# The end of a state-space stage: three C products on VectorE, gate and projection in parts, the shift on GpSimd, statistics by pairs

## What is computed

```python
def _L1_attn_ref(x_in, W_in, W_x, W_dt, b_dt, A_log, D_param, W_out, ln_g, ln_b):
    xz = x_in @ W_in
    x, z = (xz[..., :D], xz[..., D:])
    ...
    dA = jnp.exp(jnp.einsum('bld,dn->bldn', delta, A))
    dBx = jnp.einsum('bld,bln->bldn', delta * x, B_ssm)
    def step(h, inp):
        dA_t, dBx_t, C_t = inp
        h = dA_t * h + dBx_t
        y_t = jnp.einsum('bdn,bn->bd', h, C_t)
        return (h, y_t)
    ...
    y = jnp.moveaxis(ys, 0, 1) + x * D_param
    y = y * jax.nn.silu(z) @ W_out
    res = y + x_in
    ...
    return (res - mu) * jax.lax.rsqrt(var + LN_EPS) * ln_g + ln_b

h = h + _L1_attn_ref(_layernorm(h, axis=-1), ...)
h = h + _L1_ffn_ref(_layernorm(h, axis=-1), ...)
```

## Time and profile before

| | us |
|---|---|
| median of 3 runs | 739.95 |
| lowest and highest | 738.63, 740.12 |
| the profiled execution | 738.0 |
| its span, first to last instruction | 736.2 |

### The profile page before, as it was taken

One profiled execution on the slowest core, in us unless ns is written; L12 is line 12 of the kernel. 1 busy time (PEld: TensorE's weight loads), 2 busy tenths in 40 slices (PEclk: granted clock), 3 DMA queues, 4 the chain that ended last, 5 costly groups with the idle time before them and its releaser, 6 DMA issues.

```text
span 736.2 us, 15971 instructions
## 1 busy us (share of the span) xinstructions
PE 673.4 (91%) x6442; PEld 522.6 (71%) x6489; DVE 345.0 (47%) x1039; ACT 256.0 (35%) x638; POOL 140.4 (19%) x109
## 2 busy tenths in 40 slices
PE   9898899899856698999988989999999998999997
PEld 6666688795433356876754679888886556998996
DVE  3328550006999876568578642211117762211113
ACT  0433354454633505563692212222220112222221
POOL 2000110001299900130050221111110040111110
PEclk9999999999999999999999999999999999999999
DMA  8981099916465230000002889999347047899923
GB/s 306 390 285 57 16 328 381 396 64 219 148 158 145 66 130 1 0 1 1 0 2 99 317 289 344 382 358 373 138 139 305 0 169 242 340 373 357 359 97 104
DMA packets 30196, 144.97 MB, mean 197 GB/s; under 512 B 4592, under 2 KB 14640, under 8 KB 23600
## 3 DMA queue, kind: packets, MB, share of 16 engines
q1 hardware_dynamic: 26352, 136.31, 50.9%
q0 software_dynamic: 2624, 6.71, 2.6%
q10 hardware_dynamic: 1152, 0.98, 0.4%
HBM read 133.19 MB, written 10.79 MB: 196 GB/s over the span
## 4 chain that ended last, share of the span: by engine, by line
PE 66%; DVE 12%; issue 10%; DMA 4%; ACT 3%; POOL 3%; SPq 1%; DVEq 0%; ACTq 0%; POOLq 0%
PE PS L592 62%; DVE arena L2219 5%; DMA y_slots<-arena 2%; PE PS L651 2%; SPq L436 1%; DMA gatew<-gate_w 1%; PE PS L615 1%; POOL arena L1659 1%; DMA arena<-bc_scratch 1%; DVE arena L2354 1%; POOL arena L1646 1%; POOL arena L1662 1%; ACT XT L1255 1%; PE PS L1049 0%; POOL arena L1654 0%
## 5 line engine op out<-in xcount | busy, mean ns | idle before, releaser
L592 PE MATMUL PS<-arena 128*64 128x64 f32 (+4 forms) x3090 | 249.3, 264 | 11.3 <-DVE arena L2357 3.1
L592 PEld LDWEIGHTS PS<-arena 128*64 128x64 f32 (+1 forms) x3090 | 210.9, 154 | 40.3 <-issue 14.9
L1982 DVE TENSOR_TENSOR arena<-arena,PS 128x384 f32<-128x384 f32 (+1 forms) x66 | 26.8, 407 | 175.5 <-ACT arena L1299 175.5
L592 PE MATMUL PS<-warm 128*128 128x512 bf16 (+2 forms) x306 | 74.6, 352 | 5.0 <-POOL warm L1586 1.3
L1299 ACT ACTIVATE arena<-PS 128x384 f32<-128x384 f32 (+1 forms) x66 | 27.2, 413 | 135.4 <-PE PS L592 135.4
L1629 POOL DMA_INDIRECT y_tok<-arena,yto x32 | 29.7, 928 | 195.8 <-ACT arena L1316 90.5
L1646 POOL TENSOR_TENSOR arena<-arena 128x1152 f32<-128x1152 f32 x16 | 56.4, 3522 | 31.7 <-DVE arena L2219 31.6
L592 PE MATMUL PS<-arena,ident 128*128 128x512 f32 (+1 forms) x128 | 38.0, 440 | 21.5 <-POOL arena L1646 21.5
L1616 POOL DMA_INDIRECT x_slots<-XHW,posu x25 | 24.2, 966 | 166.0 <-DVE posu L1896 159.3
L592 PEld LDWEIGHTS PS<-warm 128*128 128x128 bf16 (+1 forms) x353 | 31.8, 101 | 33.3 <-issue 4.8
L592 PE MATMUL PS<-arena,wsh 128*64 128x64 f32 (+3 forms) x680 | 50.7, 249 | 3.5 <-ACT arena L1291 2.4
(11 more groups left out here) (318 smaller groups left out, 933.7 us busy)
## 6 DMA issues: line engine op xcount, KB each, us to landing
arena<-w_moe SPq DMA_DIRECT2D x24, 2176.0 KB, 10.1
arena<-w_moe SPq DMA_DIRECT2D x9, 2052.0 KB, 14.3
wsh<-w_moe SPq DMA_DIRECT2D x8, 2176.0 KB, 10.3
arena<-bc_scratch SPq DMA_DIRECT2D x32, 288.0 KB, 3.8
wsh<-w_moe SPq DMA_DIRECT2D x3, 2052.0 KB, 12.8
wx<-w_moe SPq DMA_DIRECT2D x1, 2176.0 KB, 18.8
wx<-w_sh SPq DMA_DIRECT2D x1, 2176.0 KB, 9.8
arena<-x_slots SPq DMA_DIRECT2D x2, 1032.0 KB, 6.0
```

What stands on the lines that cost most here:

```text
L592: return nc.tensor.matmul(out_, l, r, start=start, stop=stop, skip_group_check=True)
L1982: ins = v.tensor_tensor(firsts(hid_b[x][:, 0:full], n_), firsts(sg_s[x][:, 0:full], n_), firsts(PS[:, 2 * x + 1, 0:full], n_), ALU.mult)
```

## The change

The changed kernel does in the last two states and behind them:

```diff
-        Y_PARTS = [(0, slice(0, Y_CUT), PS[:, 0, 0:Y_CUT]), (1, slice(0, Y_CUT), PS[:, 1, 0:Y_CUT]),
-                   (0, slice(Y_CUT, T), PS[:, 2, 0:T - Y_CUT]), (1, slice(Y_CUT, T), PS[:, 2, T - Y_CUT:2 * (T - Y_CUT)])]
+        Y_PARTS = [(0, slice(0, Y_CUT), PS[:, 0, 0:Y_CUT]), (0, slice(Y_CUT, T), PS[:, 2, 0:T - Y_CUT]),
+                   (1, slice(Y_CUT, T), PS[:, 2, T - Y_CUT:2 * (T - Y_CUT)]), (1, slice(0, Y_CUT), PS[:, 1, 0:Y_CUT])]
...
             keep_warm(3)
-            with pe.Fori(0, NS // 2) as i:
+            with pe.Fori(0, NS // 2 - 1) as i:
...
-            idle_products(7)
-            pe.wait_ge(sem("ys_ready"), 1)
-            token_products("attn1", lambda k, j: ys[:, k, tsl(j)], KD, lambda k: wout_s[:, k, :])
-            keep_warm(12, root=6)
+            pe.wait_ge(sem("hc_done"), NS + 1)
+            for i, (d, ts, acc) in enumerate(Y_PARTS):
+                if i == 2:
+                    pe.wait_ge(sem("ys_ready"), 1)
+                last = mm(acc, ident[:, :], hC[:, 0, d, ts], False, False)
+            last.then_inc(sem("hc_read"), 1)
+            for i, (d, ts, acc) in enumerate(Y_PARTS):
+                if i in (0, 2):
+                    pe.wait_ge(sem("ys_ready"), 2 + i // 2)
+                last = mm(acc, ident[:, :], hC[:, 1, d, ts], False, True)
+                if i != 1:
+                    last.then_inc(sem("hc_read"), 1)
+            pe.wait_ge(sem("ys_ready"), 5)
+            for j in range(2):
+                mm(TM(j), ys[:, 0, tsl(j)], wout_s[:, 0, :], j == 0, False)
+            pe.wait_ge(sem("ys_ready"), 6)
+            for j in range(NT - 1):
+                for k in range(1 if j < 2 else 0, KD):
+                    last = mm(TM(j), ys[:, k, tsl(j)], wout_s[:, k, :], k == 0, k == KD - 1)
+                last.then_inc(sem("tm_ready"), 1)
+            last_tile_products(lambda k: ys[:, k, tsl(NT - 1)], lambda k: wout_s[:, k, :], KD)
+            keep_warm(11, root=6)
...
-            with pool.Fori(0, NS // 4) as i:
+            with pool.Fori(0, NS // 4 - 1) as i:
                 for n in range(4):
+                    times_C(i, n)
+            for n in range(3):
+                times_C(NS // 4 - 1, n, 4 if n < 2 else 3)
+            for q, (j, n) in enumerate(PAIRS):
+                nc.gpsimd.tensor_tensor(pair(H, q), pair(H, q), row("ln_b")[0:TILE_N[j], None, :].to_broadcast([TILE_N[j], n, D]), ALU.add)\
+                    .then_inc(sem("hc_done"), 1)
...
+            half_scan(NS - 1, 0)
+            times_C(NS - 2, 1)
+            half_scan(NS - 1, 1)
+            times_C(NS - 1, 0)
+            times_C(NS - 1, 1)
...
+            for i, (y_, src, z_) in enumerate(((ys[:, 0, 0:Y_CUT], PS[:, 0, 0:Y_CUT], zs[:, 0, 0:Y_CUT]),
+                                               (ys[:, :, Y_CUT:T], y_tail, zs[:, :, Y_CUT:T]),
+                                               (ys[:, 1, 0:Y_CUT], PS[:, 1, 0:Y_CUT], zs[:, 1, 0:Y_CUT]))):
+                dve.wait_ge(sem("hc_read"), NS + 2 + i)
+                v.tensor_tensor(y_, src, z_, ALU.mult).then_inc(sem("ys_ready"), 1)
```

More of the change, by code:

```diff
@@ L2227, in _ @@
                     scan(i, n)
-            for n in range(4):
-                if n < 3:
-                    input_of(NS // 4 - 1, n + 1)
-                scan(NS // 4 - 1, n)
-            dve.wait_ge(sem("z_silu"), 1)
[L2233 to L2236, removed]
@@ L2237, in _, with half_scan, times_C @@
-            normed_residual(3 * NT, "ln_g", "ln_b")
+            def half_scan(n, d):
+                dve.wait_ge(sem("dA_ready"), 2 * n + d + 1)
+                v.tensor_tensor_scan(hs_[:, n % 2, d], dA[d], dBx[:, n % 2, d], 0.0, ALU.mult, ALU.add)\
+                    .then_inc(sem("scan_half"), 1)
+            def times_C(n, d):
+                dve.wait_ge(sem("scan_half"), 2 * n + d + 3)
+                dve.wait_ge(sem("hc_read"), n + 1)
+                dve.wait_ge(sem(f"C{n % 4}"), 16 * (n // 4) + 16)
+                v.tensor_tensor(hC[:, n % 2, d, :], hs_[:, n % 2, d, :], bcC[:, n % 4, :], ALU.mult).then_inc(sem("ys_ready"), 1)
@@ new lines, in _ @@
+            for n in range(3):
+                input_of(NS // 4 - 1, n + 1)
+                scan(NS // 4 - 1, n)
+            dve.wait_ge(sem("dbx_done"), NS)
+            dve.wait_ge(sem("hc_done"), NS)
+            half_scan(NS - 1, 0)
[3 more added lines that the diff above has]
+            times_C(NS - 1, 1)
+            y_tail = PS[:, 2, 0:KD * (T - Y_CUT)].rearrange("p (k t) -> p k t", k=KD)
+            dve.wait_ge(sem("z_silu"), 1)
@@ new lines, in _ @@
+            for i, (y_, src, z_) in enumerate(((ys[:, 0, 0:Y_CUT], PS[:, 0, 0:Y_CUT], zs[:, 0, 0:Y_CUT]),
[3 more added lines that the diff above has]
+                v.tensor_tensor(y_, src, z_, ALU.mult).then_inc(sem("ys_ready"), 1)
+            for q in range(len(PAIRS)):
+                tile_in(3 * NT, 2 * q)
+                if q < len(PAIRS) - 1:
+                    mark(v.tensor_tensor(pair(TMP, q), TM2(q), pair(XH, q), ALU.add))
+                else:
+                    for h in range(2):
+                        hs = slice(128 * h, 128 * (h + 1))
+                        mark(v.tensor_tensor(tile(TMP, NT - 1)[:, hs], TMH(h), tile(XH, NT - 1)[:, hs], ALU.add))
+                join()
+                for j in range(PAIRS[q][0], PAIRS[q][0] + PAIRS[q][1]):
+                    tile_stats(tile(TMP, j), j)
@@ new lines, in _ @@
+            variances()
+            half_variance()
+            for j in range(NT):
+                mark(v.scalar_tensor_tensor(tile(TMP, j), tile(TMP, j), tile(mv, j)[:, 0:1], row("ln_g")[0:TILE_N[j]],
+                                            ALU.subtract, ALU.mult))
+            dve.wait_ge(sem("hc_done"), NS + 1 + len(PAIRS))
+            link(newton())
+            for j in range(NT):
+                mark(v.scalar_tensor_tensor(tile(H, j), tile(TMP, j), tile(root[0], j)[:, 3:4], tile(H, j), ALU.mult, ALU.add))
@@ L2240, in _ @@
+            all_stats(H)
             layer_norm_h()
```

16 lines of the change are left out of this document (9 added, 7 removed).

## The result

| | before | after |
|---|---|---|
| median of 6 runs each on one chip, us | 739.47 | 743.18 |
| lowest and highest | 738.43, 740.82 | 741.37, 746.33 |
| the profiled execution | 738.0 | 742.26 |
| its span | 736.2 | 740.4 |

The changed kernel is slower: the ratio is 1.0051, 95% interval [1.0029, 1.0072], some 2 to 5 us. 737.4 was forecast, with 739.1 as the upper end of the range.

The account below looks back on a forecast made before the run. VectorE's scans and GpSimd's C products set the pace until 252.5 us, then a tail runs one engine at a time. Gain 3.34 less collision 0.85 is 2.5: 735.5 profiled, median 737.4, range 735.9 to 739.1.

Parts of the forecast that it names:

- the start of the sum: Last states: the old pace holds until TensorE starts at 252.52, and GpSimd's half of product 14 runs from 252.62.
- The slower rival: GpSimd before product 12, TensorE before 14: leaving loops brings instruction waits; two of 2.19 us give median 741.8; chance 0.07.
- The new end: From TensorE's last products to the variances: variances start at 265.55 instead of 268.89, 3.34 us earlier without a collision.
- three products without a gap: TensorE's last three products follow one another from 252.52, 2.21 us each, ending at 259.15, if no source is late.
- C products 0.75: VectorE's three products by C, 576 columns each, between and behind the last scans: 0.75 us each, replacing waiting.
- first addition to variances: VectorE's pair additions and statistics beside the projection: additions start at 261.30, variances at 265.55.
- shift worth nothing: Five shift additions, 1.75 us, were done while VectorE waited for TensorE; taking them off VectorE gains nothing by itself.
- statistics by pairs: VectorE's statistics, 1.73 us in a block before: two pairs now lie in the waits for TensorE's projection.
- eleven turns enough: TensorE's warm-up loop, 11 turns instead of 12: ends at 273.48, VectorE's tiles allow 273.86, so 0.4 us to spare.
- The collision: GpSimd's shift additions beside VectorE's three C products: TensorE starts product 15 late, costing 0.85 us, bounds 0 to 2.8.
- the mild form of the rival by which GpSimd holds on: GpSimd takes its first shift addition at 254.02 without yielding: 1.4 late, gain 1.9 us, 738.0; whole rival's chance 0.14.

Follow-up runs that it names:

- e8: The changed kernel with GpSimd's products 0 and 1 written out, 2 to 13 looped, the half of 14 behind; median 738.57 us, ratio 0.9991 to the kernel before.
- e9: e8 with GpSimd's shift additions waiting until VectorE's three C products are done; median 737.74 us, ratio 0.9979 to the kernel before.
- e10: e8 with the five shift additions back on VectorE and none on GpSimd; median 736.16 us, ratio 0.9959 to the kernel before.
- e12: The changed kernel with a small GpSimd fill ahead of the written-out products 12, 13 and 14; median 738.71 us, ratio 0.9980 to the kernel before.
- e1: The changed kernel with GpSimd's products 12, 13 and 14 waiting for VectorE's next input product; median 740.46 us, ratio 1.0002 to the kernel before.
- e13: e10 run once more, unchanged, in five rounds; median 737.71 us, ratio 0.9969 to the kernel before.
- e3: The kernel before with all 16 of GpSimd's products written out; median 748.07 us, ratio 1.0118 to the kernel before.
- e14: e10 with TensorE's program nine products shorter behind the stage, as many products run; median 738.67 us, ratio 0.9978 to the kernel before.
- e15: The kernel before with TensorE's program nine products longer behind the stage, as many products run; median 741.39 us, ratio 1.0020 to the kernel before.
- e4: e3 with each GpSimd product waiting until VectorE's next input product is done; median 741.40 us, ratio 1.0015 to the kernel before.

## Why the prediction was wrong

- **The step that failed** is the start of the sum. It let the old pace run up to TensorE's start at 252.52 and laid GpSimd's half of product 14 at 252.62, as if products 12 and 13 were the old ones. They are the old ones in work, but no longer in a loop, and they start 0.02 us before VectorE in place of 0.1 behind. The sum put this at nothing. The missing term is 2 x 2.45 us on VectorE, 3.80 at the stage's end (after against e8). Both pieces of it were at hand: the rule that a VectorE product of two SBUF operands stands until GpSimd is done, and the start times of before. The rule was used at the shift alone, where GpSimd got new work, and not where the same work starts at another time.
- **The slower rival** named the place, GpSimd leaving its loop before product 12, but as a wait for instructions of 2.19. No such wait is there: GpSimd's row at 252.74 has its releaser. Waits of that kind showed at another place, in TensorE's program 450 us later, at 0.72 to 1.00.
- **The new end** was right: predicted 3.34 us without a collision, measured 94.13 - 90.68 = 3.45 (e9, e10). Its parts hold: three products without a gap 6.63, measured 6.59 in e10 (253.23 to 259.82); C products 0.75, measured 0.73; first addition to variances 4.25, measured 4.20 in e9; shift worth nothing; statistics by pairs worth some 0.5 by the sum's own times (its second pair's statistics end behind TensorE's last tile), measured 0.53, where the words had both pairs in the waits; eleven turns enough, the transposes wait for VectorE alone.
- **The collision** was right in kind, and two of its orders came true. In e12 it went as the sum had it: the first C product gets its turn, the second stands until GpSimd's second addition is done, and it costs 0.84, where 0.85 was laid down. In e8 it went as in the mild form of the rival by which GpSimd holds on, priced at 1.4: GpSimd goes from the half of product 14 to its first addition before VectorE's product (1.85), and product 15's first half waits for the third addition; it costs 1.31. GpSimd does yield between its instructions, when VectorE is there. In e8 its half of 14 followed on product 13 with no gap, where the sum had 0.15 us, and so the addition was ahead by 0.03. That the sum met 0.84 so closely is in part luck: its two start times lay within hundredths of each other.
- **Sum.** 3.45 - 1.31 - 3.80 = -1.66: the stage. The medians are 3.7 us apart. Behind the stage the trace after takes 467.7 us and before 466.8, 0.9 more; the other 1.1 stay open. Single runs of the kernel before scatter by up to 6 us (737.42 to 743.55), in part ahead of the stage, where nothing was changed, and in e1, e12 and e13 the clock fell at places behind it.
- The Trainium skill (SBUF — State Buffer, section Who interferes with whom) says that the one that issues first has the shared ports for its whole instruction. The traces agree: of 277 places where a product or addition of GpSimd and one of VectorE that reads nothing from PSUM overlap by 0.15 us or more, the one that starts later stands in 276, and the exception is the start 0.01 us ahead in e12. The page would have given the missing term, had it been asked of products 12 and 13.

## What to carry to other kernels

Where two engines that block each other are released by the same semaphore, write down who starts first and by how much, and ask of every edit, even one that only unrolls a loop, whether it turns that order round: here 0.1 us of lag was worth 3.8 us. Compare parts between two marks inside the traces where single runs differ by more than the change, and look at places behind the change too: a program that grows by a few instructions moves the waits that belong to places in it, and what that costs in sum is known only from all parts together.

The version that beats both kernels is the change with GpSimd's loop laid over products 2 to 13 and the shift left on VectorE (e10, e13): 736.16 and 737.71 us, 0.3 to 0.4% under the kernel before.

## What was not expected of the hardware

- GpSimd starts 0.08 us behind its releaser where the product is written out, 0.22 to 0.27 in a loop whose waits are computed (before, after, e8); VectorE 0.10 in written-out code and 0.03 in its loop (it is first there, by 0.04, in e3). Between blocking engines that decides which of them loses: GpSimd 1.1 us (3.7 for 2.6), or VectorE 2.45 (3.81 for 1.36). Why a loop's lag differs so was not tried.
- TensorE's waits without a releaser in the last two layers, 0.33 to 2.43 us, belong to places in its program (e14, e15). The Trainium skill (Runtime: NRT & Kernel Launch, section Instruction fetch mechanics) calls the loading of the next block mostly hidden. If these waits are that loading, it is not hidden here; why the position of before costs nothing near 700 us stays open.
- TensorE's clock fell to 0.50 in a wait of 3.98 us in the stage after, and is 1.00 beside the waits of 1.5 of every state in e8 to e10. In e4 it stayed at 1.00 beside ten waits of 1.62 and fell behind one of 1.99. In the third layer it fell behind a wait of 1.98 (e12) and one of 2.04 (e1), and not behind one of 2.01 (e15). So the length of the wait alone does not tell whether it falls.
